# Local attention in a two-layer AdaLN network: probabilities one unit later, the maximum as a bias, projections from split operands

## What is computed

```python
h = shift_token(x)                      # x: 4 sequences of 1024 tokens, 128 features
q, k, v = split(h @ wqkv)               # 128 -> 3 x 512, 8 heads of 64
q = l2norm(q) * qs;  k = l2norm(k) * ksc
q, k = rotary_xpos(q, k)
sim = einsum('bhwid,bhwjd->bhwij', q * 8.0, k_with_previous_window)   # windows of 64, 128 keys
attn = softmax(where(mask, -max, sim)); o = attn @ v_with_previous_window
x = x + o @ wo
h = layernorm(shift_token(x)) @ w1 + b1
x = x + (a * gelu(g)) @ w2 + b2         # a, g = halves of h
```

## Time and profile before

| | |
|---|---|
| median of 3 runs | 1565.78 us (1561.47 to 1570.25) |
| profiled execution, whole | 1563.58 us |
| its span, first to last instruction | 1561.7 us |
| busy in the span | PE 1346.8, DVE 1145.6, ACT 801.7, POOL 724.0 us |
| mean granted clock of TensorE | 0.947 of full |
| the stage touched | from about 705 us to the end |
| one unit in the steady state | 9.85 us |

### The profile page before, as it was taken

The page is one execution under the profiler, slowest core; times in us unless marked ns, Lnnn a source line. Parts: engine busy times, 40 slices in busy tenths (PEclk is TensorE's granted clock), DMA queues, the critical chain, the costliest instruction groups (busy, mean ns, idle before and its releaser), DMA issues.

```text
span 1561.7 us, 39029 instructions
## 1 busy us (share of the span) xinstructions
PE 1346.8 (86%) x15968; PEld 970.4 (62%) x15968; DVE 1145.6 (73%) x2484; ACT 801.7 (51%) x1633; POOL 724.0 (46%) x562
## 2 busy tenths in 40 slices
PE   4545999988999999984999999967989999998797
PEld 3434878875777777762666666654556666665554
DVE  3776776434888888874888888864578888888565
ACT  1222223224666666653777777742457777776421
POOL 1752545541344433434666666632246666666100
PEclk7776999996999999997999999999999999999999
DMA  4000544500000000003000100011100000000011
GB/s 133 0 0 16 112 93 110 108 13 2 3 3 3 4 3 3 3 3 91 8 8 7 22 8 8 1 30 28 25 24 8 9 17 13 9 5 2 12 31 54
DMA packets 61837, 40.34 MB, mean 26 GB/s; under 512 B 41312, under 2 KB 51808, under 8 KB 61664
## 3 DMA queue, kind: packets, MB, share of 16 engines
q1 hardware_dynamic: 61664, 37.88, 10.2%
HBM read 27.12 MB, written 2.36 MB: 19 GB/s over the span
## 4 chain that ended last, share of the span: by engine, by line
PE 33%; ACT 8%; SPq 6%; DVE 4%; POOL 2%; issue 1%; DMA 1%; DVEq 0%; POOLq 0%; ACTq 0%
PE PS L1872 7%; SPq L1463 5%; PE PS L1923 5%; PE PS L1957 4%; PE PS L1914 4%; PE PS L1891 3%; PE PS L1937 2%; ACT e_oT L1787 2%; PE PS L1948 2%; ACT qk L1756 2%; ACT e_pm L1793 2%; PE PS L1907 2%; POOL rot L1537 2%; PE PS L2010 1%; PE PS L2019 1%
## 5 line engine op out<-in xcount | busy, mean ns | idle before, releaser
L1537 POOL TENSOR_TENSOR rot<-qk,sinl 128x1024 f32<-128x1024 f32 x64 | 217.6, 3401 | 139.4 <-DVE qk L1631 139.4
L1530 POOL TENSOR_TENSOR rn<-ss,neghalf 128x16 f32<-128x16 f32 x64 | 185.6, 2901 | 108.6 <-DVE ss L1624 108.6
L1756 ACT ACTIVATE qk<-PS 128x512 f32<-128x512 f32 x128 | 76.4, 597 | 135.7 <-PE PS L1872 135.7
L1102 DVE TENSOR_REDUCE d_mx<-PS 128x4 f32<-128x576 f32 x128 | 96.9, 757 | 66.3 <-PE PS L1246 63.3
L1872 PE MATMUL PS<-wqkv,hT 128*128 128x512 f32 x256 | 128.8, 626 | 10.9 <-DMA qks<-in_e_ks 5.7
L607 POOL TENSOR_TENSOR uu<-uu,cb 128x512 f32<-128x512 f32 x64 | 82.8, 1295 | 90.0 <-DVE uu L839 88.2
L1923 PE MATMUL PS<-ident,e_pm 128*128 128x128 f32 x512 | 84.5, 289 | 45.9 <-ACT e_pm L1793 44.3
L1923 PEld LDWEIGHTS PS<-ident,e_pm 128*128 128x128 f32 x512 | 55.9, 144 | 102.4 <-ACT e_pm L1793 95.7
L739 ACT ACTIVATE sg<-PS 128x512 f32<-128x512 f32 x72 | 43.0, 597 | 134.1 <-PE PS L667 133.0
L1165 ACT ACTIVATE pa<-PS 128x512 f32<-128x512 f32 x128 | 76.5, 597 | 61.8 <-PE PS L1255 61.7
L1610 DVE TENSOR_REDUCE e_mx<-PS 128x8 f32<-128x1024 f32 x64 | 78.2, 1222 | 30.7 <-PE PS L1914 30.6
(11 more groups left out here) (241 smaller groups left out, 3535.9 us busy)
## 6 DMA issues: line engine op xcount, KB each, us to landing
cb<-comb_rows SPq DMA_DIRECT2D x32, 512.0 KB, 9.1
X<-in_L_attn_x SPq DMA_DIRECT2D x4, 512.0 KB, 7.4
zs<-Z SPq DMA_DIRECT2D x64, 32.0 KB
zg<-Z SPq DMA_DIRECT2D x16, 128.0 KB
out_x<-X SPq DMA_DIRECT2D x8, 256.0 KB, 2.5
zs<-Z SPq DMA_DIRECT2D x64, 31.8 KB
zg<-Z SPq DMA_DIRECT2D x16, 127.0 KB
wqkv<-in_e_wqkv SPq DMA_DIRECT2D x2, 768.0 KB, 4.2
```

Source lines behind the costliest of these rows:

```text
L1102: chain(dve.tensor_reduce(mx[:, par, :, :], s, AX.X, ALU.max))
L1530: pool.tensor_tensor(rn[:, v % 2, :], ss[:, v % 2, :], c.neghalf[:, :], ALU.pow).then_inc(rn_ready.sem, 1)
L1537: pool.tensor_tensor(rot[:, :, :, :], x, bc(sinl[:, t, :, :], 2, H2), ALU.mult).then_inc(rot_ready.sem, 1)
L1756: last = act.activation(qk[:, v % 4, s, :, :].rearrange("p h e -> p (h e)"), PS[:, QBANK + s, :], ACT.Copy)
```

## The change

- **Projections.** `wqkv` is split once a layer into `w_hi` (rounded to float32r by ACT) and `w_lo` (the remainder, by DVE in layer 0 and POOL in layer 1). The features are split for each unit: `features` writes `h_hi`, a new DVE instruction `low` writes `h_lo`. Each of the three projections becomes three float32r products into one accumulation.
- **Softmax.** `shift` becomes `maxima`: the row maximum, negated, into `mx`. The subtraction is gone. `exponent` reads the scores from PSUM and adds `mx` as the bias operand; a bias holds one value for each partition, so there are eight calls of 128 columns where there were two of 512. The PSUM banks of the scores are free for `scores(u+1)` only when the last of these is done.
- **Order.** `turn_p`, `weigh`, `divide` work on unit u-1, `turn_o`, `project_o`, `resid_sum` on u-2, `project_v` on u+2. ACT deals its calls out anew; `features(u+5)` now stands behind `take_qk(u+1)` and ahead of `squares`. A step `attend(L, nunits)` is added at the end of each layer, with `up(L, 0, 0)` on PE inside it.
- `zero` and `mask32` now lie in `c.hT`, and the wait of `load_projections` changes accordingly.

```diff
+        w_hi, w_lo = ssb("wqkv_hi", [P, 3 * INNER], F32R), ssb("wqkv_lo", [P, 3 * INNER], F32R)
+        h_hi, h_lo = ssb("e_h_hi", [P, 4, P], F32R), ssb("e_h_lo", [P, 4, P], F32R)
...
-                        sp.wait_ge(ev_psum.sem, ev_psum.at(nunits * L))
+                        sp.wait_ge(wlo_ready.sem, wlo_ready.at(3 * L))
...
+                def split_weights(L, k):
+                    pool.wait_ge(whi_ready.sem, whi_ready.at(3 * L + k + 1))
+                    pool.tensor_tensor(w_lo[:, third(k)], wqkv[:, third(k)], w_hi[:, third(k)], ALU.subtract).then_inc(wlo_ready.sem, 1)
...
-                def shift(L, v):
+                def low(L, v):
+                    dve.wait_ge(eh_ready.sem, eh_ready.at(n(L, v)))
+                    dve.tensor_tensor(h_lo[:, v % 4, :], PS[:, QBANK, 0:P], h_hi[:, v % 4, :], ALU.subtract).then_inc(el_ready.sem, 1)
+
+                def maxima(L, v):
                     dve.wait_ge(s_ready.sem, s_ready.at(n(L, v)))
+                    if n(L, v) > 2:
+                        dve.wait_ge(p_exp.sem, p_exp.at(2 * (n(L, v) - 2)))
                     s = PS[:, SBANK:SBANK + 2, :].rearrange("p r (j k) -> p r j k", k=2 * W2)
-                    steps(dve.tensor_reduce(mx[:, :, :], s, AX.X, ALU.max))
-                    for h in range(2):
-                        if n(L, v) > 2:
-                            dve.wait_ge(pT_psum.sem, pT_psum.at(2 * (n(L, v) - 2) - 1 + h))
-                        dve.tensor_tensor(pm[:, v % 2, h, :, :, :], s[:, :, 2 * h:2 * h + 2, :],
-                                          bc(mx[:, :, 2 * h:2 * h + 2], 3, 2 * W2), ALU.subtract).then_inc(p_shifted.sem, 1)
+                    dve.tensor_reduce(mx[:, v % 2, :, :], s, AX.X, ALU.max, negate=True).then_inc(max_ready.sem, 1)
...
                 def attend(L, u):
+                    if has(u + 4) and (u >= 0 or L == 0):
+                        low(L, u + 4)
                     if has(u):
-                        shift(L, u)
+                        maxima(L, u)
                     if u == nunits - 3:
...
-                    if has(u):
-                        divide(L, u, 0)
+                    if has(u - 1):
+                        divide(L, u - 1, 0)
                     if has(u + 2):
                         rotated(L, u + 2)
                     if has(u + 3):
                         clamp(L, u + 3)
-                    if has(u):
-                        divide(L, u, 1)
                     if has(u - 1):
-                        resid_sum(L, u - 1)
+                        divide(L, u - 1, 1)
+                    if has(u - 2):
+                        resid_sum(L, u - 2)
...
+                for k in range(3):
+                    dve.wait_ge(whi_ready.sem, whi_ready.at(k + 1))
+                    dve.tensor_tensor(w_lo[:, third(k)], wqkv[:, third(k)], w_hi[:, third(k)], ALU.subtract).then_inc(wlo_ready.sem, 1)
...
+                    attend(L, nunits)
                     resid_sum(L, nunits - 1)
                     dve.wait_ge(w_loaded.sem, w_loaded.at(16 * 5 * (L + 1)))
                     for g in range(G):
+                        if L + 1 < DEPTH and lead(g) is not None:
+                            low(L + 1, lead(g) + 4)
...
-                    act.activation(h_of(v), PS[:, QBANK, 0:P], ACT.Copy).then_inc(eh_ready.sem, 1)
-
-                def take_features(L, v):
-                    for s in range(2):
-                        act.wait_ge(eqkv_ready.sem, eqkv_ready.at(2 * n(L, v) - 1 + s))
-                        last = act.activation(qk[:, v % 4, s, :, :].rearrange("p h e -> p (h e)"), PS[:, QBANK + s, :], ACT.Copy)
-                    last.then_inc(qk_taken.sem, 1)
+                    act.activation(h_hi[:, v % 4, :], PS[:, QBANK, 0:P], ACT.Copy).then_inc(eh_ready.sem, 1)
+
+                def round_weights(L, k):
+                    if k == 0:
+                        act.wait_ge(qkv_loaded.sem, qkv_loaded.at(16 * 3 * (L + 1)))
+                        if L:
+                            act.wait_ge(ev_psum.sem, ev_psum.at(nunits * L))
+                    act.activation(w_hi[:, third(k)], wqkv[:, third(k)], ACT.Copy).then_inc(whi_ready.sem, 1)
+
+                def take_features(L, v, s):
+                    act.wait_ge(eqkv_ready.sem, eqkv_ready.at(2 * n(L, v) - 1 + s))
+                    act.activation(qk[:, v % 4, s, :, :].rearrange("p h e -> p (h e)"), PS[:, QBANK + s, :],
+                                   ACT.Copy).then_inc(qk_taken.sem, 1)
...
-                def exponent(L, v, h):
-                    act.wait_ge(p_shifted.sem, p_shifted.at(2 * n(L, v) - 1 + h))
-                    p = pm[:, v % 2, h, :, :, :].rearrange("p r j k -> p (r j k)")
-                    act.activation(p, p, ACT.Exp).then_inc(p_exp.sem, 1)
+                def exponent(L, v, h, r):
+                    if h == 0 and r == 0:
+                        act.wait_ge(max_ready.sem, max_ready.at(n(L, v)))
+                    if n(L, v) > 2 and r == 0:
+                        act.wait_ge(pT_psum.sem, pT_psum.at(2 * (n(L, v) - 2) - 1 + h))
+                    for j in range(2):
+                        at = 2 * h + j
+                        last = act.activation(pm[:, v % 2, h, r, j, :], PS[:, SBANK + r, at * KEYS2:(at + 1) * KEYS2], ACT.Exp,
+                                              bias=mx[:, v % 2, r, at:at + 1])
+                    if r == 1:
+                        last.then_inc(p_exp.sem, 1)
...
                 def attend(L, u):
                     if has(u + 4):
-                        if u >= 0 or L == 0:
-                            features(L, u + 4)
-                        take_features(L, u + 4)
+                        take_features(L, u + 4, 0)
                     if has(u):
-                        exponent(L, u, 0)
-                        exponent(L, u, 1)
-                        take_p(L, u, 0)
-                    if has(u + 3):
-                        values(L, u + 3)
+                        exponent(L, u, 0, 0)
+                    if has(u + 4):
+                        take_features(L, u + 4, 1)
+                    if has(u - 1):
+                        take_p(L, u - 1, 0)
+                    if has(u):
+                        exponent(L, u, 0, 1)
+                    if has(u + 2):
+                        values(L, u + 2)
                     if u == nunits - 1:
                         whole(L, 0)
+                    if has(u - 1):
+                        take_p(L, u - 1, 1)
                     if has(u):
-                        take_p(L, u, 1)
-                    if has(u - 1):
-                        take_o(L, u - 1)
+                        exponent(L, u, 1, 0)
+                    if has(u - 2):
+                        take_o(L, u - 2)
+                    if has(u):
+                        exponent(L, u, 1, 1)
                     if has(u + 1):
                         take_qk(L, u + 1)
+                    if has(u + 5) and (u >= -1 or L == 0):
+                        features(L, u + 5)
                     if has(u + 4):
                         squares(L, u + 4)
...
+                for k in range(3):
+                    round_weights(0, k)
+                features(0, 0)
...
+                        if L + 1 < DEPTH and g < 3:
+                            round_weights(L + 1, g)
...
+                def project(to, v, k):
+                    pe.matmul(to, h_hi[:, v % 4, :], w_hi[:, third(k)], start=True, stop=False)
+                    pe.matmul(to, h_hi[:, v % 4, :], w_lo[:, third(k)], start=False, stop=False)
+                    return pe.matmul(to, h_lo[:, v % 4, :], w_hi[:, third(k)], start=False, stop=True)
+
                 def project_qk(L, v):
-                    pe.wait_ge(eh_ready.sem, eh_ready.at(n(L, v)))
-                    if v == 0:
-                        pe.wait_ge(qkv_loaded.sem, qkv_loaded.at(16 * 3 * (L + 1)))
+                    pe.wait_ge(el_ready.sem, el_ready.at(n(L, v)))
                     for s in range(2):
-                        pe.matmul(PS[:, QBANK + s, :], h_of(v), wqkv[:, s * INNER:(s + 1) * INNER],
-                                  start=True, stop=True).then_inc(eqkv_ready.sem, 1)
+                        if v == 0:
+                            pe.wait_ge(wlo_ready.sem, wlo_ready.at(3 * L + s + 1))
+                        project(PS[:, QBANK + s, :], v, s).then_inc(eqkv_ready.sem, 1)
...
-                        pe.wait_ge(p_shifted.sem, p_shifted.at(2 * n(L, v - 1)))
+                        pe.wait_ge(p_exp.sem, p_exp.at(2 * n(L, v - 1)))
...
                         scores(L, u)
                     if has(u + 4):
                         project_qk(L, u + 4)
-                    if has(u + 3):
-                        project_v(L, u + 3)
+                    if u == nunits:
+                        up(L, 0, 0)
+                    if has(u - 1):
+                        turn_p(L, u - 1, 0)
+                    if has(u + 2):
+                        project_v(L, u + 2)
```

(37 more changed lines are left out.)

11 lines of the change are left out of this document (6 added, 5 removed).

## The result

The changed kernel takes 1571.53 us (median of 14 executions, 1565.89 to 1573.74), the kernel before beside it on the same chip 1565.99 us (14 executions, 1560.27 to 1570.25): a ratio of 1.0032, 95% interval 1.0018 to 1.0047. It is 3 to 7 us slower, inside the 0.5% called "within", and 0.5 us from the forecast. What follows compares these two profiles part by part.

A forecast was written before the change was run, and what follows sets the result against it. A serial loop through ACT and PE was to bound the changed kernel's unit at 9.81 us. -2.1 + 5.6 - 0.8 + 2 x (-2 + 3.9) + 0 = +6.5 us on 1563.6: 1570, in medians 1572, range 1555 to 1589.

The forecast's parts named there:

- The loop: Steady unit: a serial loop through ACT and PE, `scores` to `scores`, takes 9.81 us instead of 9.85.
- The exponential's step: ACT: an exponential of 128 columns with bias, from PSUM, steps 0.26 us, range 0.16 to 0.29.
- Rival 1: ACT: exponentials step 0.29 us, unit 9.95, whole 1579 us; at worst 0.375 and 1596; chance 0.23, of it 0.04 worst.
- The units in sum: 52 steady units of both layers: 0.04 us less each, -2.1 us in all.
- The start: Layer 0: first projection waits for `low` behind DVE's tables, 5.9 us later; net +5.6 us, range 4 to 6.
- the 0.4 of filling: Part of the term for filling and the start of layer 1: -0.8 us, range -2 to +1.
- The last units: Units 28 to 31: about 9.1, 9.2 and 11.3 us, plus 1 for a slow clock; -2 us a layer.
- The tail: `scores(31)` to the second `up`, each layer: 17.2 us instead of 13.3, +3.9 a layer.
- The feed-forward: Feed-forward part of layer 0: paced by loads, `rstd` of two groups delayed 1 to 2 us; 0, range -1 to +3.
- Rival 2: Steady unit: loop not serial, POOL and DVE bound at 9.1 us; whole 1536 us, or 1554 for half; chance 0.15.
- Rival 3: PE's clock falls now and then in the units, about 3 us per slow unit; 1600 us; chance 0.04.
- Rival 4: Projections: float32r products as slow as float32, unit 10.1 us, whole 1585 us; chance 0.02.

The follow-up runs named there:

- experiment 1: Changed kernel with the last pair of exponentials moved ahead of `take_o` in ACT's order: 1544.77 us, ratio to the kernel before 0.9874.
- experiment 2: Changed kernel with the exponentials' bias operand left out, so the maximum is computed but not subtracted: 1551.71 us, one execution.
- experiment 5: Changed kernel with `low(0, 0)` ahead of DVE's tables instead of behind them: 1567.77 us, ratio to the kernel before 1.0010.
- experiment 6: Changed kernel with last exponentials ahead of `take_o`, `low(0)` ahead of the tables, first `up` between `turn_o(31)` and `project_o(31)`: 1536.35 us, ratio to the kernel before 0.9822.
- experiment 3: Kernel before with the split float32r projections alone, softmax and order as before: 1564.78 us, ratio to the kernel before 1.0000.
- experiment 4: Changed kernel with the float32 projections of the kernel before, no split and no `low`: 1571.74 us, ratio to the kernel before 1.0054.
- experiment 7: Kernel of experiment 6 with `turn_qk(u+1)` ahead of `turn_p(u-1, 1)` on PE: 1529.01 us, ratio to the kernel before 0.9773.

## Why the prediction was right, step by step

- **The loop.** Right in kind and, to 0.03 us, in size. Its marks from the start of `scores`, walk against trace: ACT starts at 2.55 and 2.56 (866.36 - 863.80), the end of the first `take_p` 4.65 and 4.65, `take_o` 7.52 and 7.54, `scores(u+1)` 9.81 and 9.84. Two errors inside partly cancel: pairs of exponentials step 0.50, not 0.52, and from the end of `take_p` to the start of `turn_p` it is 868.59 - 868.45 = 0.14 us, not 0.05. Experiments 1 and 2 show the loop: with one pair taken off it the unit is 9.33, and to shorter exponentials it answers with two pairs of the four.
- **The exponential's step.** 0.25, taken as 0.26 from the copy's 0.16 and the Gelu's 0.095. Rival 1 took the Exp from SBUF as its base, 0.20; from PSUM it is 0.155. The page of the Trainium skill "Perfetto Trace Analysis", section "Optimizing Scalar/DVE Operations", puts the overhead of ScalarE at about 93 ns on SBUF and about 51 on PSUM; the difference of 0.042 agrees with the 0.20 and 0.155 here. The rule that was weighed in the prediction ("ScalarE: Activation LUTs", section "What ACT_TABLE_LOAD costs") is met by the durations, 0.379 us for one with bias against the 0.386 that it gives for 128 columns (an estimate from that page), but successive ones overlap by 0.13 us here, not 0.093, and so its 0.29 is too long.
- **The units in sum.** -0.04 a unit was forecast, -0.01 came (9.844 to 9.835): -0.4 us for 48 units instead of -1.9.
- **The start.** The wait behind the tables was +5.7, forecast +5.9. Mis-sized: the 0.3 us that shorter products were to give back, and the 0.4 of filling. From the first projection to scores(4) nothing is gained, and in layer 1 the first four units cost 0.5 us. The first triple steps 0.59 and 0.43 us there (722.49, 723.08, 723.50) where it steps 0.34 and 0.23 in the steady state. Also, the step saw one cause where two lie close together: with `low` ahead of the tables, 2.1 of the 5.7 us remain (experiment 5).
- **The last units.** -2 a layer became -0.6 and -1.5. The first two are as walked (9.11 each, against 9.1 and 9.2). In the third the "plus 1 for a slow clock" is the term that was too small: after the stop of 4.18 us, `turn_p` to the start of `project_o` takes 1051.55 - 1045.73 = 5.8 us, in a steady unit 871.99 - 868.59 = 3.4, so the clock cost 2.4 us in layer 0, and likewise 1.5 in layer 1 (1468.87 - 1463.93 = 4.9).
- **The tail.** 1070.18 - 1052.82 = 17.36 us, forecast 17.2: +4.05 a layer, +3.9 forecast. By experiment 6 the place of the first `up` accounts for 1.0 us of it.
- **The feed-forward.** 0, range -1 to +3, was forecast. Of layer 0 the table gives +2.6 with the tail of 4.05 in it, so -1.5, just outside the range: from the second `up` to `scores(0)` of layer 1 it is 93.00 us instead of 94.48. The shorter projections are not the cause. With them alone the stretch is 95.65 (experiment 3), and with the rest of the change and without them 92.55 (experiment 4), so the gain comes with softmax and order. DVE's waits for `rstd` that were foreseen are there, but of 0.65 and 0.50 us, not 1 to 2. Where exactly in softmax and order it lies, no run isolates.
- **Sum.** +6.5 forecast. By the medians +5.5 (3 to 7 by the interval), by the profiled executions +10.2; the latter compares the slowest of 14 with one below its median. The parts of the table miss by 3.7 us in sum, where the median misses by 0.5; that the whole came so close is in part luck. Single executions of one kernel differ by up to 10 us, so no term below 2 us could have been checked by the whole time. They could by the traces: the steady units agree to 0.1 us in 236 between executions (236.05 in after, 236.01 in the kernel of experiment 5).
- **The rivals.** 1 falls by the step of 0.25, and the unit was not 9.95. 2 falls for the change as it stands: PE had 0.8 us of idle time and could use none. Experiments 1 and 7 show that this time can be had in part, but only by an order that shortens the loop. Of the bound of 9.1 us that it put on DVE and POOL the kind is right and the size 0.1 short: their loop steps 9.19 us where it runs at its own pace (experiment 7), since 0.09 us pass between the end of the power and the normalisation, where the walk had nothing. No kernel was held by it in the steady state, the shortest unit being 9.24. 3 did not happen in the steady state (clock 1.00), only at the edges. 4 falls: two triples take 866.85 - 865.36 = 1.49 us, as in the earlier trace rows.

## What to carry to other kernels

When two engines hand one unit's work to and fro, walk from a step to its next occurrence through both in-order lists, and put a number on each link; busy shares tell nothing here. Then look in each list for work that stands behind an instruction which waits for the other engine, although it doesn't need it: moving two exponentials ahead of such a one was worth 25 to 27 us, while shortening three products by a fifth of their time was worth 0.16 us a unit, and 6 us of the whole. And cost the first and last units of a pipeline by themselves: here the change won 0.4 us in 48 steady units and lost some 10 us, by the profiles, in all the rest.

## What the runs showed of the hardware

- ACT, source in PSUM: an Exp of 128 columns steps 0.155 us, with a bias from memory 0.25; the bias costs 0.095 us with 128 columns, and as much with the Gelu's 512 if a Gelu without one steps like a copy (0.58 - 0.485).
- TensorE's clock at the edges: in the 10 us with the 4.18 us stop the mean granted clock is 0.73 (its line in the table of stretches of after stands below), so part of it ran at the lower of the two levels, and PE's groups are slow for some 6 us after work resumed (a set of 16 products 1.14 us). The same stop of 2.15 us in the same place left the clock high in the kernel before (16 products 0.69 us) and low in that of experiment 3 (1.14 us), which cost the latter over 2 us.

```profile
1040.00:1050.00 10.00, 5.82 (x66) 4.98 (x64) 4.60 (x16) 2.75 (x8) 1.27 (x3) 0.73 0.05 11
```

- From the end of an ACT instruction to the start of the PE instruction that it releases, 0.05 us before `project_o` and `turn_z`, but 0.14 before the second `turn_p` (868.59 - 868.45), in the change and in experiments 1, 4, 5 and 6 alike. Why was not found.
